# Warm-up transposes placed before a late load, and two batches of queries moved from VectorE to ScalarE

## The reference, cut to what matters

```python
x = x + tanh(g_xattn[0]) * xattn(ctx, ctx, layernorm(x), ssm_kernel, D, 8)
# xattn, per head: kv = k_i * v_j (8x8 pairs), convolved along the positions with ssm_kernel,
# + kv * D, times q_i, summed over i
x = x + tanh(g_ffn[0]) * ffn(layernorm(x), ...)     # top 2 of 8 experts, gelu, projection
```

## Time and profile before

| what | us |
|---|---|
| median of 3 runs | 113.68 |
| lowest and highest of the 3 | 113.64 and 114.54 |
| the profiled execution, first to last instruction (span) | 112.1 |
| TensorE busy with matmuls in it | 104.3 |
| VectorE busy | 89.6 |
| ScalarE busy | 57.7 |
| GpSimd busy | 61.8 |

### The profile page before, as it was taken

One profiled execution on the slowest core, in us unless ns is written; L12 is line 12 of the kernel. 1 busy time (PEld: TensorE's weight loads), 2 busy tenths in 40 slices (PEclk: granted clock), 3 DMA queues, 4 the chain that ended last, 5 costly groups with the idle time before them and its releaser, 6 DMA issues.

```text
span 112.1 us, 1945 instructions
## 1 busy us (share of the span) xinstructions
PE 104.3 (93%) x586; PEld 89.4 (80%) x586; DVE 89.6 (80%) x295; ACT 57.7 (51%) x145; POOL 61.8 (55%) x82
## 2 busy tenths in 40 slices
PE   4946999999999999999999999999999999999970
PEld 4936988788989977867788888887788888888960
DVE  0166699999999999999999979688189987767860
ACT  4051749265418095674469697965444352442510
POOL 4015798999999959999999999900000000000000
PEclk9996799999999999999999999999999999999999
DMA  2845999557837451003000000000000111010122
GB/s 68 266 153 168 264 369 337 175 146 213 249 114 223 137 152 49 0 3 94 0 6 0 0 0 0 0 0 0 0 0 6 47 47 27 19 50 11 36 60 80
DMA packets 11091, 10.00 MB, mean 89 GB/s; under 512 B 1314, under 2 KB 11082, under 8 KB 11082
## 3 DMA queue, kind: packets, MB, share of 16 engines
q1 hardware_dynamic: 9570, 8.78, 26.5%
q10 hardware_dynamic: 1512, 1.12, 3.3%
HBM read 8.82 MB, written 1.07 MB: 88 GB/s over the span
## 4 chain that ended last, share of the span: by engine, by line
PE 50%; DVE 22%; POOL 12%; DMA 7%; issue 5%; ACT 1%; SPq 1%; DVEq 0%; POOLq 0%
PE ring L878 11%; PE ring L880 11%; PE ring L879 11%; DVE zq_t L1065 6%; POOL zq_t L419 5%; DVE zq_t L1067 5%; DMA ctx_t<-in_ctx 4%; PE red L819 3%; DVE kv_t L387 3%; DMA dcol<-in_L_xattn_D 2%; DVE zq_t L1070 2%; DVE zq_t L1069 2%; PE red L745 2%; PE zbank L922 2%; POOL kv_t L387 2%
## 5 line engine op out<-in xcount | busy, mean ns | idle before, releaser
L1165 DVE SCALAR_TENSOR_TENSOR mix_t<-ring,ctxT_t,mix_t 128x256 f32<-128x256 f32 x53 | 25.4, 482 | 6.0 <-ACT ring L633 4.3
L633 ACT ACTIVATE ring<-ring 128x512 f32<-128x512 f32 (+1 forms) x32 | 18.1, 567 | 18.6 <-PE ring L880 18.5
L387 POOL TENSOR_TENSOR kv_t<-ctxT_t 128x320 f32<-128x320 f32 x25 | 21.5, 886 | 8.4 <-ACT ctxT_t L545 6.0
L878 PE MATMUL ring<-w_hi_t,zT_hi_t 128*128 128x512 f32 (+1 forms) x64 | 25.5, 399 | 0.0
L880 PE MATMUL ring<-w_hi_t,zT_lo_t 128*128 128x512 f32 (+1 forms) x64 | 24.6, 384 | 0.0
L879 PE MATMUL ring<-w_lo_t,zT_hi_t 128*128 128x512 f32 (+1 forms) x64 | 24.6, 384 | 0.0
L795 PE MATMUL ring<-kv_t,toep_t 128*128 128x288 f32 x64 | 21.4, 416 | 0.0
L796 PEld LDWEIGHTS ring<-kv_t,toep_t 128*128 128x128 f32 x64 | 12.2, 190 | 3.4
L880 PEld LDWEIGHTS ring<-w_hi_t,zT_lo_t 128*128 128x128 f32 x64 | 12.0, 188 | 2.5
L878 PEld LDWEIGHTS ring<-w_hi_t,zT_hi_t 128*128 128x128 f32 x64 | 12.0, 188 | 2.2
L879 PEld LDWEIGHTS ring<-w_lo_t,zT_hi_t 128*128 128x128 f32 x64 | 12.1, 189 | 1.9
(11 more groups left out here) (139 smaller groups left out, 182.4 us busy)
## 6 DMA issues: line engine op xcount, KB each, us to landing
ctx_t<-in_L_ffn_expert_w SPq DMA_DIRECT2D x8, 256.0 KB, 4.3
toep_t<-kpad_dram SPq DMA_DIRECT2D x3, 512.0 KB, 6.7
x_t<-in_x SPq DMA_DIRECT2D x8, 128.0 KB
out<-x_t SPq DMA_DIRECT2D x7, 128.0 KB
wlast_t<-in_L_ffn_expert_w SPq DMA_DIRECT2D x1, 768.0 KB, 6.3
ctx_t<-in_ctx ACTq DMA_DIRECT2D x2, 256.0 KB, 3.1
zq_t<-in_x ACTq DMA_DIRECT2D x2, 256.0 KB, 4.6
ctx_t<-in_ctx SPq DMA_DIRECT2D x2, 256.0 KB, 4.7
```

Of the source, the lines that this page charges most:

```text
L387: eng.tensor_tensor(dst, head.unsqueeze(1).to_broadcast([P, HB + 1, HD * CB]), windows(ctxT_t, g, h, HB + 1), ALU.mult).then_inc(done, 1)
L633: act.activation(y, y, ACT.Gelu_apprx_tanh).then_inc(gelu_ready, 1)
L878: pe.matmul(y, hi, whi, start=(c == 0), stop=False)
L1165: dve.scalar_tensor_tensor(out=acc, in0=block_bank(n)[:, L * e:L * (e + 1)], scalar=gate, in1=acc, op0=ALU.mult, op1=ALU.add).then_inc(mix ...
```

## The change

`WARM_UP` becomes 24 behind the second context load and 1 in front of the queries. `first_queries` on VectorE makes the queries of batches 0 and 1 only, and in front of them the shifts `-mean * qscale` of batches 2 and 3. ScalarE makes the queries of batches 2 and 3 behind `half_gains`, in front of its copies of group 1's contexts. GpSimd waits for two first queries instead of four. TensorE's `queries(1)` waits for a semaphore of its own.

```diff
-WARM_UP = (12, 1, 6, 1, 5, 1)
+WARM_UP = (12, 1, 24, 1, 1, 1)
...
-                pool.wait_ge(first_queries_ready, BG)
+                pool.wait_ge(first_queries_ready, BL)
...
             def queries(i):
-                act.wait_ge(shifts_ready, 1)
+                if i == 1:
+                    act.wait_ge(first_shifts_ready, 1)
+                else:
+                    act.wait_ge(shifts_ready, 1)
+                done = second_queries_ready if i == 1 else late_queries_ready
                 for b in range(BL * i, BL * (i + 1)):
                     act.activation(backwards(q_t, B * L, b * L), xn[:, b, :].rearrange("p (c n) -> p c n", c=C),
                                    ACT.Identity, scale=qscale[:, b:b + 1],
-                                   bias=shift[:, b:b + 1]).then_inc(late_queries_ready, 1)
+                                   bias=shift[:, b:b + 1]).then_inc(done, 1)
...
             half_gains()
+            queries(1)
             for c in range(C):
                 evacuate(ctxT, red, context_transposed, 1, c, context_evacuated)
...
-                if i < 2:
-                    pe.wait_ge(first_queries_ready, BL * (i + 1))
+                if i == 0:
+                    pe.wait_ge(first_queries_ready, BL)
+                elif i == 1:
+                    pe.wait_ge(second_queries_ready, BL)
...
+            def second_shifts():
+                own = slice(BL, BG)
+                dve.wait_ge(first_query_scales_ready, 1)
+                dve.scalar_tensor_tensor(out=shift[:, own], in0=mvv[:, own, 0], scalar=-1.0, in1=qscale[:, own],
+                                         op0=ALU.mult, op1=ALU.mult).then_inc(first_shifts_ready, 1)
...
             def first_queries():
                 query_scales()
+                second_shifts()
                 queries(0)
-                queries(1)
```

More of the change, by code:

```diff
@@ L223, in flamingo_kernel @@
         late_queries_ready = sem("late_queries_ready")
+        second_queries_ready = sem("second_queries_ready")
         z_ready = sem("z_ready")
@@ L242, in flamingo_kernel @@
         first_queries_ready = sem("first_queries_ready")
+        first_shifts_ready = sem("first_shifts_ready")
         dve_queries_evacuated = sem("dve_queries_evacuated")
```

## The result

The kernel with the change takes **113.07 us** in the median of 21 runs (112.62 to 113.39). The kernel before takes 113.68 in as many (112.88 to 114.86). The ratio is 0.9942, with an interval of 0.9924 to 0.9961: faster by 0.4 to 0.8%, which this many runs can tell from no change, though it is under the 1% of the prediction's bound.

What follows compares the result with a forecast made beforehand. The prediction took the chain from the second context load through transposes, queries and VectorE's products, then GpSimd and TensorE, as the bound. -0.54 (VectorE) and -0.23 (GpSimd) gave -0.77: 113.68 to 112.9 us, 8-in-10 range 112.4 to 114.1.

Steps and rivals of the forecast that it cites:

- the likeliest case: The forecast itself, 112.9 us with a range of its own of 112.6 to 113.2; chance 0.4.
- The warm-ups hold the clock: TensorE before the third load: 24 warm-ups end at 8.83, idle falls from 2.45 to 0.5 us, clock stays up.
- The queries on ScalarE: Hand-over: ScalarE's two queries start at 10.70, its last copy ends at 14.04, VectorE's first product follows at 14.10.
- What is next: Behind the hand-over: convolution 6 at 17.01 instead of 17.78, GpSimd's scales at 20.50 instead of 21.27, 0.77 us gained.
- VectorE's -0.54: Hand-over: VectorE's first product at 14.10 instead of 14.64, -0.54 us.
- a lead of GpSimd of -0.23: At VectorE's products 25 and 27, which follow GpSimd: its further lead comes through, -0.23 us, bounds 0 and 0.23.
- I carry the change of the span over to the median: Whole kernel: profiled span 112.1 us taken as typical, 1.58 us below the median 113.68, so both change alike.
- The first rival: Clock does not fall in a typical execution of before: VectorE +0.42, GpSimd nothing, 113.7 to 114.1 us; chance 0.2.
- third: Rival: clock falls in the new TensorE gaps around the queries, slowing convolutions; 114.1 to 114.5 us; chance 0.08.
- fourth: Rival: the head's gain is lost where VectorE's and GpSimd's products wait for each other; 113.3 to 113.7 us; chance 0.12.
- fifth: Rival: ScalarE's part is shorter, VectorE's first product at 13.5, GpSimd's scales at 20.3; 112.5 to 112.7 us; chance 0.1.

Runs made afterwards that it cites:

- e1: The kernel before with 24 warm-ups behind the second context load, still 5 in front of the queries and no moved queries: 113.35 us, ratio 0.9993.
- e2: The changed kernel with 6 warm-ups behind the second context load instead of 24, still 1 in front of the queries: 114.35 us, ratio 0.9986.
- c0: The kernel before, run once more unchanged: 113.60 us, ratio 1.0001.
- e4: The changed kernel with ScalarE's copies of the transposed queries in front of its copies of group 1's contexts: 112.93 us, ratio 0.9928.
- e6: The changed kernel with VectorE repeating the larger of its two query copies behind ScalarE's last one: 114.03 us, ratio 1.0037.
- f0: The changed kernel, run once more unaltered: 113.17 us, ratio 0.9924.
- e3: The kernel before with the change's warm-ups, 24 and 1, and four queries on VectorE as before: 113.38 us, ratio 0.9974.
- f8: The kernel before with warm-ups 24 and 1, no moved queries, and GpSimd waiting for two queries instead of four: 113.60 us, ratio 0.9971.
- f9: The changed kernel with GpSimd waiting for ScalarE's two queries as well, four in all: 113.12 us, ratio 0.9927.

## Why the prediction was right, and where it was not

The forecast was 112.9 us; 113.07 was measured, inside the likeliest case's own range. The size of the step between the two profiles came out, but two of its reasons did not. That the median came so close is in part luck: the spans explain half of its fall, and the other half has no known cause (5).

1. **The warm-ups hold the clock: right.** The granted clock is 1.00 in all three stretches, and the page shows it lower only in its last slice, when TensorE has no work left; 2 of 124 executions of kernels with 24 warm-ups had a low mean clock, against 54 of 123 of the kernel before. The size was off: 24 took 3.35 us where I had 2.8, since the step fell to 0.11 us later in this execution; they ended at 9.53, not 8.83, and the transposes of the third load began at 9.36 (9.31 in before). That nothing but transposes raises and holds the clock goes against the rule of the Trainium skill ("TensorE: Matmul & The Clock Gate", Part 4, PE-mode transpose) that was weighed there. Two pairs of kernels that differ in 18 transposes alone show the holding: e1 beside before (a low clock in 0 of 12 executions against 54 of 123) and the change beside e2 (0 of 33 against 8 of 12). The earlier trace rows show the rise.

2. **The queries on ScalarE: right, each row 0.1 to 0.2 late.** The shifts started at 10.65 (10.46 in the forecast, GpSimd's deviations were 0.2 later), ScalarE's two took 1.09 as worked out, its contexts started at 11.85 (11.70), its last copy ended at 14.16 (14.04) and VectorE's first product came at 14.19 (14.10), behind ScalarE as said.

3. **"What is next": right up to GpSimd, wrong in the sum.** The seventh convolution (16.92 for 17.01) and the scales (20.41 for 20.50) came as forecast. But I wrote the sum as VectorE's -0.54 plus a lead of GpSimd of -0.23. The runs show one term: what GpSimd gains is what the end gains. c0 has VectorE 0.38 ahead of the change and is 0.3 longer; e4 moves VectorE half a microsecond ahead and gains about 0.1; e6 moves it 0.86 back, and GpSimd and the end go with it.

4. **The step that failed: "I carry the change of the span over to the median."** I took the profiled execution, with its fall, for a typical one. It was at the long end: 112.1, where the median span of before is 111.6 and under half of its executions fall. Against a typical span of the runs beside the experiments the change gains 0.3, not 0.77. The first rival named just this, and its clock was right more often than not (69 of 123 executions), so 0.2 was far too little for it. Its price was wrong as well: it gave "nothing for GpSimd" and called the change slower. In an undisturbed execution the seventh convolution does come at the same time either way (16.94 and 16.92), but GpSimd's product 12 does not wait for it there, as it is held up by product 3, which ran into VectorE's products. Taking two queries off VectorE ends those products 0.55 earlier. I had the same collision in the earlier trace rows at 35 us, and did not look for it at 12.

5. **What the median gained beyond the spans stays open.** The spans account for 0.3 of the 0.61 us. The rest lies between the device time and the span. That difference is 1.8 us in most executions. It is above 2.1 in 51 of 111 runs of before beside the experiments, but in 2 of 12 in c0, which is the same code; with the change it is so in none of the 21 executions, but in 3 of 12 in f0, again the same code. So it does not seem to follow the code, I found no cause, and this part of the 0.61 may not be the change's. c0's ratio of 1.0001 says that the comparison as a whole carries no bias of this size, but with an interval of 0.4% to either side.

6. The other rivals: the clock did not fall in the new gaps (third), the gain was not lost in the later meetings (fourth: -0.86 at the scales, -0.75 at the fold), and nothing beyond the forecast came (fifth).

## What to carry to other kernels

Before a gain read from one profiled execution is carried over to the median, ask whether that execution is typical: here the list of spans and mean clocks over the runs, or a second profile of the unchanged kernel, would have halved the forecast. To find the engine that sets the end, look for the point behind which the time to the end is the same in every variant; an earlier start of any other engine is only worth what arrives there. Discarded transposes in a gap that waits for a load kept the clock up at no cost that could be measured (e1, e3). They gained nothing by themselves either; what speaks for them is that with 6 of them instead of 24 the changed kernel (e2) was 2.5 to 3 us longer in three of 12 executions and once 39 us longer, at a low clock each time.

## What the hardware showed

- **Whether the clock falls differs from execution to execution.** The same code has a low mean clock in 54 of 123 executions. The profiled fall of 3.3 us came behind a gap of 2.45 us on TensorE, yet in e2 a gap of 2.87 us was followed by 1.00. An execution with a low clock has 0.3 to 0.4 us more span; in e2 means of 0.963 to 0.966 came with spans of 113.5 to 114.1, and one of 0.663 with 150.0.
- **VectorE and GpSimd block each other's products.** A GpSimd product takes 0.83 alone and 1.42 beside VectorE's; VectorE's two take 0.89 alone, 1.52 in f8 and 3.09 at 35 us in before. The one that comes second waits rather than sharing: in the change product 3 ends when f9's does, though it starts 0.55 earlier. The Trainium skill ("SBUF — State Buffer", Who interferes with whom) calls it a lock on a shared pair of ports, for which a VectorE instruction with two inputs from SBUF contends with a GpSimd instruction that reads SBUF; the rows agree.
- In f8 a query of VectorE, which reads one large tile and two values per row, was held up beside GpSimd too: the fourth, begun at 10.76 while GpSimd's product ran from 10.60 to 11.53, took 0.92 instead of 0.41. The other three took what they always take.
